# Moving the first quantising pass over x from ScalarE to GpSimd in the gate and up stage

## The reference, cut to what matters

```python
def _act_fake_quant(x, clip_factor):
    scale = jax.nn.sigmoid(clip_factor) * jnp.max(jnp.abs(x)) / QMAX
    return jnp.clip(_ste_round(x / scale), -QMAX - 1.0, QMAX) * scale
...
xq = _act_fake_quant(x, clip_x[0])
gate = jnp.einsum('bsh,ih->bsi', xq, _weight_fake_quant(w_gate))
up = jnp.einsum('bsh,ih->bsi', xq, _weight_fake_quant(w_up))
h = _act_fake_quant(jax.nn.silu(gate) * up, clip_down[0])
return jnp.einsum('bsi,hi->bsh', h, _weight_fake_quant(w_down))
```

## Time and profile before

| | |
|---|---|
| median of 3 runs | 659.41 us |
| span of the profiled execution, first to last instruction | 656.6 us |
| busy PE, DVE, ACT, POOL | 602.6, 514.8, 440.1, 441.8 us |
| mean granted TensorE clock | 0.970 |

### The profile page before, as it was taken

How to read it: one execution, slowest core, us unless ns; L and a number is a source line. 1 busy time by engine, 2 the same in 40 slices (tenths; PEclk the granted TensorE clock), 3 DMA queues, 4 the chain that set the end, 5 groups by cost and what they waited for, 6 DMA issues and landing times.

```text
span 656.6 us, 15688 instructions
## 1 busy us (share of the span) xinstructions
PE 602.6 (92%) x4478; PEld 412.7 (63%) x4482; DVE 514.8 (78%) x1361; ACT 440.1 (67%) x744; POOL 441.8 (67%) x597
## 2 busy tenths in 40 slices
PE   7998888999994487999999999999999999999995
PEld 2343335766762265677777777777777777777774
DVE  5579995899997887888888888888776666666653
ACT  3759995998964456888787787777665444555542
POOL 4116560187885986888888888878878677666544
PEclk8979999999996798999999999999999999999998
DMA  8522001346448238999898999978996666666552
GB/s 268 205 51 87 1 0 50 97 133 211 146 134 272 90 52 183 237 194 201 179 187 164 190 165 193 198 121 111 153 162 115 112 111 109 109 111 116 100 91 33
DMA packets 149378, 89.35 MB, mean 136 GB/s; under 512 B 106788, under 2 KB 142260, under 8 KB 149300
## 3 DMA queue, kind: packets, MB, share of 16 engines
q1 hardware_dynamic: 134596, 68.77, 47.0%
q0 software_dynamic: 14080, 19.54, 18.0%
q10 hardware_dynamic: 624, 0.03, 0.1%
HBM read 44.68 MB, written 18.40 MB: 96 GB/s over the span
## 4 chain that ended last, share of the span: by engine, by line
PE 51%; DVE 24%; issue 8%; DMA 7%; ACT 5%; SPq 2%; POOL 2%; POOLq 1%; DVEq 0%; ACTq 0%
PE ps L689 27%; PE ps L740 14%; DMA small<-small 3%; PE ps L545 2%; DVE big L1552 2%; DVE big L1394 2%; PE ps L668 2%; DVE small L1191 2%; DVE big L1201 1%; DVE small L1265 1%; PE ps L563 1%; PE ps L540 1%; DVE small L1243 1%; DVE small L1510 1%; DMA big<-in_Wu 1%
## 5 line engine op out<-in xcount | busy, mean ns | idle before, releaser
L689 PE MATMUL ps<-big,small 128*128 x1608 | 251.7, 313 | 1.9 <-ACT small L970 1.3
L689 PEld LDWEIGHTS ps<-big,small 128*128 128x128 f16 x1608 | 156.9, 98 | 80.4 <-issue 3.8
L1731 POOL DMA_INDIRECT out<-small x67 | 107.4, 1603 | 75.5 <-DVE small L1519 73.7
L740 PE MATMUL ps<-big,small 128*128 x1105 | 131.3, 273 | 0.6 <-DMA small<-small 0.6
L740 PEld LDWEIGHTS ps<-big,small 128*128 128x128 f16 x1105 | 105.2, 98 | 12.2 <-issue 1.0
L976 ACT ACTIVATE small<-small 128x704 f16<-128x704 f32 x67 | 52.6, 785 | 77.7 <-DVE small L1494 71.6
L1510 DVE SCALAR_TENSOR_TENSOR small<-small 128x64 f16<-128x64 f32 (+1 forms) x134 | 72.6, 583 | 20.5 <-ACT small L980 14.4
L1699 POOL DMA_INDIRECT small<-rows,small x67 | 75.8, 1131 | 11.8 <-issue 10.6
L1494 DVE SCALAR_TENSOR_TENSOR small<-ps,small 128x704 f32<-128x704 f32 x67 | 63.5, 947 | 25.0 <-issue 13.2
L980 ACT ACTIVATE small<-small 128x704 f16<-128x704 f32 x67 | 59.1, 882 | 28.0 <-DVE small L1504 28.0
L1707 POOL TENSOR_SCALAR small<-small 128x1 f32<-128x1 f32 x67 | 69.7, 1040 | 0.0
(11 more groups left out here) (266 smaller groups left out, 1068.5 us busy)
## 6 DMA issues: line engine op xcount, KB each, us to landing
big<-in_Wg SPq DMA_DIRECT2D x8, 704.0 KB, 6.2
big<-in_Wu SPq DMA_DIRECT2D x8, 704.0 KB, 8.4
big<-in_Wd SPq DMA_DIRECT2D x8, 640.0 KB
rows<-small SPq DMA_DIRECT2D x8, 518.0 KB, 5.0
big<-in_xT SPq DMA_DIRECT2D x8, 512.0 KB, 7.0
small<-in_xT SPq DMA_DIRECT2D x16, 256.0 KB, 4.5
out<-big SPq DMA_DIRECT2D x16, 256.0 KB, 4.3
small<-rows,small POOLq DMA_INDIRECT x67
```

The source lines that it names most:

```text
L689: m = e.matmul(ps[:, 2 * j + h, 0:352], xsT_(t)[:, 2 * xp + k, :], bigh[:, bass.ds(o + (4 * j + 2 * wp + k) * I + 352 * h, 352)], start=(n ...
L740: m = e.matmul(ps[:, 7, 0:H], hTE_(t)[:, hc_, :], bigh[:, bass.ds(o + 8 * I + (6 * wp + c) * H, H)], start=(n == 0), stop=(n == len(terms) ...
L1731: e.indirect_dma_start(out=out[:, :], out_offset=bass.IndirectOffsetOnAxis(ap=IT[:, t:t + 1], axis=0), in_=yw_(t), in_offset=None, compute ...
```

## The change

`quantise_x` goes from ScalarE's function to GpSimd's. Batch 0 stays on ScalarE. On GpSimd batch 1 stands ahead of the first product, and batch n // 6 + 2 behind product n = 6b + 2 of batches 0 to 5, two products behind a batch's first. The new form waits for the scale itself (`sc`), and has a semaphore of its own, `xmp`, on which `clip_x` waits. The arithmetic is the same multiplication and addition on the same 1024 elements per partition, in place.

```diff
@@ ScalarE @@
-            def quantise_x(b):
-                w.wait_ge("cT", 2 * b + 2)
-                e.activation(cT[:, b, :], cT[:, b, :], ACT.Copy, bias=MAGIC, scale=sc[:, 1:2]).then_inc(S["xm"], 1)
...
-                if c == 0 and b + 1 < NB:
-                    quantise_x(b + 1)
@@ VectorE @@
             def clip_x(b):
-                w.wait_ge("xm", b + 2)
+                w.wait_ge("xmp", b)
                 w.wait_ge("gu", 6 * (b - 1))
@@ GpSimd @@
+            def quantise_x(b):
+                w.wait_ge("cT", 2 * b + 2)
+                w.wait_ge("sc", KX)
+                e.tensor_scalar(cT[:, b, :], cT[:, b, :], sc[:, 1:2], MAGIC, ALU.mult, ALU.add).then_inc(S["xmp"], 1)
...
+            quantise_x(1)
             for n in range(0, 6 * NB, 2):
                 products(n)
+                if n % 6 == 2 and n // 6 + 2 < NB:
+                    quantise_x(n // 6 + 2)
```

More of the change, by code:

```diff
@@ L244, in build_program @@
         names = ("const edge ids wg wu wr wd clip gb lt pad par rgp xbp wt pt pc gu pd px hd ad rk htopp xp gate up dn "
-                 "gt tT cT wev sig xm sil ub w2g hy hu x1 relu sq bsc ex w2s hsum hhi xhi sg ha hhi2 "
+                 "gt tT cT wev sig xm xmp sil ub w2g hy hu x1 relu sq bsc ex w2s hsum hhi xhi sg ha hhi2 "
                  "wq mx rg sc cs xb xq prod prodp hmx dg one hq x1T yl vpe g rstd aff lgt rt df oh place pos route "
```

## The result

The changed kernel takes 666.99 us (median of 4 runs, 665.73 to 668.0) against 659.39 (4 runs, 659.19 to 659.68): a ratio of 1.0102, with an interval of 1.0073 to 1.0132. It is 7.6 us slower, where 10.2 had been forecast. The profiled execution has a span of 664.1 us and itself took 665.73, so an execution takes 1.6 us around its span.

A forecast was written before the change was run, and what follows sets the result against it. VectorE was taken as the bound; start +0.4, clips of batch 1 0, batch 2 +1.0, batches 3 to 6 +6.9, batch 7 +1.9 gave +10.2 on 656.6, plus 2.8: 669.6 us, range 663 to 684 (8 in 10).

The forecast's parts named there:

- rival 2: GpSimd's product comes later than at ScalarE's limit, so a batch loses one wait, not two: about +5, 664 us; chance 0.09.
- rival 4: No VectorE clip meets GpSimd, VectorE's pace stays, the early meeting may go too: -1.1 us, 658.3; chance 0.08.
- The bound: VectorE, at 6.41 us a batch against ScalarE's 6.18, sets the stage's end; shifts count one to one.
- The removed passes: ScalarE loses seven passes of 1.04 us, 7.3 us in all; gain put at nothing, since VectorE's work covers it.
- The length of the pass: Q, one added GpSimd pass of 1024 elements: taken as 1.2 us, near the copy's 1.046.
- The meeting of one batch: GpSimd's product starts 0.35 us before VectorE's first clip; the two clips wait 0.82 and 0.9, losing 1.7 us.
- rival 1: GpSimd keeps its turn between instructions, so the first clip waits 3.3 us in five batches: +20.5, 680 us; chance 0.17.
- Clips of batches 3 to 6: 4 x 1.7 = +6.9: VectorE's clips in these four batches each lose both waits, 1.7 us a batch, +6.9 us together.
- batch 7's +1.9: Clip of batch 7: no pass behind the product, so the second clip meets the next product instead: +1.9 us.
- rival 3: TensorE's clock falls, matmuls slow down, up to 1.5 us in six batches on top: +19, 679 us; chance 0.06.
- The start: The pass over batch 1 holds GpSimd until about 41.0 us, delaying VectorE's clip of batch 0: +0.4 us.
- The part around the span: The 2.8 us by which the median of the runs lies above the profiled span, added to 666.8.

The follow-up runs named there:

- a3: The changed kernel, with GpSimd's product c = 2 waiting until both VectorE clips of the next batch are done: 658.37 us, ratio 0.9986.
- a4: The changed kernel, with eight more TensorE matmuls, results unread, ahead of the up matmuls of c = 5: 667.78 us, ratio 1.0138.
- b1: The changed kernel, with ScalarE doing the lower clip as a ReLU with bias, leaving VectorE one clip in place of two: 657.47 us, ratio 0.9963.
- b4: The kernel before, with VectorE's reduction, scale and first pass over the down weights moved ahead of the stage: 655.0 us, ratio 0.9919.

## Why the prediction was right, and where it was off

**The result against the forecast.** The 666.99 us lie in the range of 663 to 684, but below the 668 to 678 that the forecast gave for its own case, between its 669.6 and the 664 of rival 2. Batches 4 and 5 came as forecast, and so did the single wait of batch 2; batches 3 and 7 lost one wait in place of two, as in rival 2; batch 6 lost none, as in rival 4. So the kind of loss was right, and how often it comes was not.

**The bound** held. VectorE has next to no idle time between 54 and 95 us in either kernel (0.2 us), and the growth of its own waits, 6.7 us, is the growth of the stage.

**The removed passes are worth nothing**: held. In a3, where the later meetings are gone, VectorE's period is the old 6.41 us, and the time is 0.14% below the kernel before, inside the interval. That run is rival 4 brought about by a wait. That it came out at rival 4's time (658.3 worked out, 658.37 measured) is in part luck: the one meeting that rival 4 counted is gone, but four other places at the start changed as well, by -0.98, +0.38, +0.16 and +0.94 us.

**The length of the pass**: taken 1.2 us, measured 1.11 to 1.14 where nothing delays it (1.11 at 40.45, 1.13 in a3). The copy was the right neighbour, the row of 128 elements with its 3.4 ns each was not. The Trainium skill (GPSIMD Engine Reference, Engine selection) calls one-input work on GpSimd "roughly line-rate"; the trace agrees, with 1.11 beside the copy's 1.046.

**The meeting of one batch**: right in each part, in batches 4 and 5. Product 0.35 ahead of the clip (0.35 measured), first clip 1.5 (1.46), second 1.3 (1.23), loss 1.7 (1.58).

**GpSimd does not keep its turn** (rival 1): the queued pass yields to the waiting clip. It lasts 1.56 in place of 1.13 behind that clip, and the clip waits for the product alone. The Trainium skill (SBUF — State Buffer, Who interferes with whom) lets issue order decide; these rows agree, unlike the earlier trace rows.

**The step that failed** is the term "Clips of batches 3 to 6: 4 x 1.7 = +6.9" and with it batch 7's +1.9 (by the prediction's own working 1.8). They measured 4.1 and 0.97. Two things were wrong in them. The forecast let the two waits begin with the clips of batch 3, with the product 0.35 us ahead of the clip; there it came 0.13 behind it, and in a4, at full clock, 0.04 behind. Only from batch 4 on was it ahead (0.35 and, in a4, 0.36). And I had said that the clock would stay at 1.00 between 50 and 100 us. It fell, as rival 3 had it, but rival 3 priced the fall as a loss of up to 1.5 us a batch on top. It had the wrong sign: with TensorE late, ScalarE loses its lead, the product comes behind the clips, and batch 6 loses nothing; batch 7 then loses one wait. Where the clock is held up, batches 4 to 7 lose 1.61, 1.60, 1.61 and 1.87 us, close to the sum's 1.7 and 1.9. That the whole stage of a4 (9.57 us) is so close to the 10.2 is luck in part: batch 3 falls 0.7 short, and the start loses about 0.9 that was not in the sum.

**The start**: +0.4 for the clip of batch 0 was right (0.37). That the products then hold one VectorE instruction more ahead of the clip of batch 1 was not foreseen (0.75 in the profile of the changed kernel); batch 1, put at 0, gained 0.36 in return. The down weights' last pass meets a product in both kernels. Batch 2, put at +1.0, lost 0.82.

**The part around the span**: I added 2.8 us, the distance of the median from one span. The profiled executions with a time of their own take 1.6 to 1.7 us around their span, so the span of before belonged to an execution about 1 us under its median. The sum isn't touched, since it goes by differences.

## What to carry to other kernels

Of two engines that both look full, find the one with the longer period before relieving the other: here VectorE takes 6.41 us a batch and ScalarE 6.18, and taking 1.04 us a batch off ScalarE bought nothing. What it did change is when ScalarE's customers run; ask of each, here GpSimd's products, what it will newly stand beside on the bound engine. If it meets there, an explicit wait of the engine that has time to spare (a3) costs nothing, and moving work off the bound engine (b1), or into its earlier idle time (b4), is what brings a gain.

## What the hardware showed that was not expected

- A VectorE instruction of only two float32 elements per partition waits beside a GpSimd product: 0.92 us, begun 0.40 behind the product's start, in place of 0.17. Its size does not protect it.
- A fall of TensorE's clock shortened the stage, by 2.9 us between the profiles of a4 and of the changed kernel, by putting an engine behind it out of step with a collision.
- TensorE was idle for 2.53 us ahead of 73.99 and for 2.54 ahead of 82.00; the granted clock stayed at 1.00 behind the first and fell behind the second. The length of one idle gap alone does not tell, in this trace, whether the clock falls.
